# Running the first model's batches while the second model's weights are prepared

## Chip, cores and metric

One core of a Trainium2 chip runs one program on five engines: TensorE (PE), VectorE (DVE), ScalarE (ACT), GpSimd (POOL) and SyncE (SP), which only issues DMAs. Each engine works off its own instructions in their written order and waits on semaphores. The metric is the device time of one execution in microseconds (us).

## What is computed

Sixteen batches `x[b]` of 256 tokens by 256 features pass through two transformer blocks with conditioning, one after the other. Cut to what matters:

```python
# model 1, float32: cond = [t, c] @ Wc + bc -> a1, g1, be1, a2, g2, be2
h = layernorm(x) * (1 + g1) + be1
x = x + a1 * (softmax(h @ Wq @ (h @ Wk).T / 16) @ (h @ Wv))
h = layernorm(x) * (1 + g2) + be2
x = x + a2 * gelu(gelu(h @ W1 + b1) @ W2 + b2)          # W1: 256 x 1024, W2: 1024 x 256
# model 2: every linear has ternary weights and 8-bit activations
scale = 1 / max(mean(abs(w)), 1e-5); wq = clip(round(w * scale), -1, 1) / scale
# conditioning, once for all batches: six layers in a row on 16 rows
h = L(wa0, silu(c)); h = L(wa2, silu(gate) * y of L(wa1, h)); h = rmsnorm(L(wa3, h) + ba3)
s_msa, sc_msa, g_msa, s_mlp, sc_mlp, g_mlp = split(L(wa4, h) + ba4)   # wa4: 1536 x 1536
mx = layernorm(x) * (1 + sc_msa) + s_msa
i, f, g = L(wi, mx), sigmoid(L(wf, mx)), L(wg, mx)
o = scan over tokens of (f, silu(i) * (1 - f));  x = x + g_msa * L(wo, rmsnorm(o) * silu(g))
m = layernorm(x) * (1 + sc_mlp) + s_mlp;         x = x + g_mlp * L(wm2, silu(gate) * value of L(wm1, m))
```

Model 1 needs nothing of model 2's weights. Model 2 needs all six rows of its conditioning, and these need the mean of all of `wa4` before the first of its weights can be rounded.

## The kernel before

**Preparation.** It runs once, before the batches, and is written out by hand on each engine. SP loads the weights into `arena1` in groups (`load_group`, L321): `wa0` and `wa1`, then `Wc`, then `wa2` and `wa3`, then the block's own weights; after these, in place of them, the 12 chunks of `wa4` (128 x 1536 each, `wa4_chunk`, L294). For each weight there are three steps: a sum of absolute values (`absum_of`, ACT L561 or DVE L1117), summed over partitions by a matmul with ones (L1512) into `wmean` and `winv`; a multiplication by `winv` and addition of 12582912 that rounds (`w_round`, ACT L566 or POOL L414); and two operations of DVE that subtract this and clip (`ternary`, L1138 and L1140). The six conditioning layers (`LAYERS`) run between these steps, DVE doing their quantising (L1231 to L1248) and outputs, and the last one, `wa4`, takes its 12 chunks as they become ternary (L1573). Model 1's attention for batch 0 alone (`EARLY`) is woven into this by hand. At the end rows for all batches go to DRAM (`rows1_d`) and are read back per batch (`load_rows1`, `load_rows2`).

**Batches.** `run_pipeline` walks one list, `SCHEDULE`, of about 120 parts, each with a lag: in step k, part (name, lag) does batch k - lag. Model 1's parts have lags 0 to 3 (it ends with `x3`, DVE L945), model 2's first half lags 4 and 5 (`mx_a`, DVE L840, to `x4`), its second half lags 5 and 6 (to `x5`, POOL L518, and `store`). Steps 0 to 7 and the last six are written out; steps 8 to 15 are a loop on each engine with two steps per turn. `x3` has two buffers (`x3_sum` waits for `x4_ready` of two batches back, L944), so model 1 can't be more than two batches ahead of `x4`.

TensorE work per batch of model 1, all float32: 8 matmuls each for q (L1339), k (L1339), v, scores and attention output (L1346), 32 up (L1392), 32 down (L1401), each on 256 columns, and 16 transposes (L1326). Model 2's matmuls are bf16 (L1346, L1474), its transposes float16 and float32.

Of the kernel before, what the change touches and what calls it, by code (L numbers as in the profile page):

```python
# [5 lines left out]
SCHEDULE = [  # L6
    ("mx_a", 4), ("so_rstd", 5), ("sq_so", 5), ("q_mm", 2), ("vv", 5), ("k_mm", 2), ("u0", 6), ("silu0", 6),
    ("qT", 2), ("sq_o", 5), ("ln3_rstd", 4), ("z_o", 5), ("silu1", 6), ("gates1", 6), ("kT", 2), ("mx_b", 4),
    ("o_rstd", 5), ("z_i", 4), ("am_o", 5), ("u1", 6), ("xn2T", 3), ("quant_o", 5), ("val1", 6), ("a_rstd", 4),
    ("h2T", 3), ("gates2", 6), ("u2", 6), ("z_f", 4), ("am_i", 4), ("int_o", 5), ("u3", 6), ("am_f", 4), ("am_g", 4),  # L10
# [4 lines left out]
    ("v_mm", 2), ("load_x", 0), ("v", 2), ("u_rstd", 6), ("qT_f", 4), ("z_m", 5), ("down0", 3), ("qT_g", 4),  # L15
    ("g1", 3), ("int_f", 4), ("m_rstd", 5), ("round_i", 4), ("probT_mm", 2), ("my_b", 5), ("am_u", 6),
# [3 lines left out]
    ("quant_m", 5), ("sq_m", 5), ("ln2_rstd", 2), ("int_u0", 6), ("forget", 4), ("int_u3", 6), ("av_mm", 2),  # L20
# [4 lines left out]

EARLY = ("load_x", "load_rows0", "ln1_moments", "ln1_rstd", "ln1_norm", "xb", "xn1T", "hT", "q_mm", "qT", "k_mm", "kT",
         "v_mm", "v", "s_mm", "score_max", "exp", "probT_mm", "probT", "av_mm", "row_sums", "x2")


class Batch:


    def __init__(self, i, parity):
        self.i, self.p = i, parity

    def back(self, k):
        return Batch(self.i - k, (self.p + k) % 2)


def column(b):
    return slice(b.i, b.i + 1) if isinstance(b.i, int) else bass.ds(b.i, 1)


def wait(eng, sem, b, k=1, n=1, unit=1):

    value = b.i * (n * unit) + k * unit
    if isinstance(value, int) and value <= 0:
        return  # L50
    eng.wait_ge(sem, value)


def wait_dma(eng, sems, b):

    value = (b.i - b.p) * 8 + 16
    if isinstance(value, int) and value <= 0:
        return
    eng.wait_ge(sems[b.p], value)


def run_pipeline(eng, parts, schedule, nb):


    most = max(lag for _, lag in schedule)

    def step(k, parity):
        for name, lag in schedule:
            if isinstance(k, int) and (not 0 <= k - lag < nb or k == lag and name in EARLY):
                continue  # L70
            if name in parts:
                parts[name](Batch(k - lag, (parity + lag) % 2))

    first = most + 2
    first += (nb - first) % 2
    for k in range(first):
        step(k, k % 2)
    with eng.Fori(first, nb - 1, 2) as i:
        for w in range(2):
            step(i + w, (first + w) % 2)  # L80
    for k in range(nb, nb + most):
        step(k, k % 2)


def build_program(nc, t):
# [4 lines left out]
    P = 128  # L90
# [13 lines left out]
    with ctx:  # L104
# [29 lines left out]
        nrow = {n: sb("row_" + n, [P, D]) for n in ("ni", "nf", "ng", "ngn", "no", "nm1")}  # L134
        nrow["nm2"] = sb("row_nm2", [P, H])
# [18 lines left out]
        arena0 = sb("arena0", [P, 14752])  # L154
        arena1 = sb("arena1", [P, 18432])
# [15 lines left out]
        LOW, HIGH = 9 * T * D, 9 * T * D + 8608  # L171
        xin, rows0 = [take2(0, T, D)], [take2(0, 2, D)]
        xb, xn1, hT, qT, kT, v, prob = (take2(0, T, D) for _ in range(7))
        assert used[0] == LOW
        rows0.append(take2(0, 2, D))
        xn2, h2T = take2(0, T, D), take2(0, T, D)
        g = take2(0, HC, S)
# [110 lines left out]
        def tern_of(j):  # L288
            n = WNAMES[j]
            if n in AW:  # L290
                return AW[n]
# [1351 lines left out]
```

## Time and profile before

| | us |
|---|---|
| Time, median of 3 executions (lowest, highest) | 789.7 (788.61, 791.23) |
| The profiled execution's own time | 789.95 |
| Its span, first to last instruction | 788.1 |
| PE, DVE, ACT, POOL busy | 628.5, 620.6, 568.3, 458.3 |
| Share of PE, DVE, ACT, POOL | 80%, 79%, 72%, 58% |

The profile is of one execution. Busy time is the time in which at least one instruction of an engine was running; matmuls are pipelined, so that the ends of two neighbours overlap. PEclk is the share of its full clock that TensorE was granted: 1.0 is 2.4 GHz, 0.5 is 1.2 GHz.

### The profile page before, as it was taken

The page shows a single profiled execution, that of the slowest core. Times are in us where ns is not written, and L with a number is a line of the kernel's source. Part 1 is how long each engine was busy: PE and PEld are TensorE (multiplying, and loading weights), DVE is VectorE, ACT ScalarE, POOL GpSimd, SP SyncE. Part 2 cuts the span into 40 slices and gives each one's busy share as a digit, 9 for nine tenths or more (in the row PEclk, how much of TensorE's full clock was granted, in tenths as well). Part 3 has the DMA queues.
Part 4 walks back from the last instruction along what each step waited for, and adds up shares of the span by engine and source line. Part 5 has one row for each costly group of instructions (what it writes and reads, how often), then busy time and mean ns, then how long its engine had stood idle before and what let it go on. Part 6 is the DMA issues. An engine that isn't in the chain of part 4 may idle for free.

```text
span 788.1 us, 13091 instructions
## 1 busy us (share of the span) xinstructions
PE 628.5 (80%) x3560; PEld 487.7 (62%) x3588; DVE 620.6 (79%) x1432; ACT 568.3 (72%) x1206; POOL 458.3 (58%) x647
## 2 busy tenths in 40 slices
PE   0631336899899999999999999999999998874552
PEld 0110212678777878888787878788888877642321
DVE  3779888223768999999899989998899889888653
ACT  1234670447689999898989999998989888774431
POOL 2203360213647686867767686867678586856623
PEclk9955579799999999999999999999999999985866
DMA  8495800111010101202021011112021010110100
GB/s 312 150 408 204 297 0 25 30 38 47 1 68 35 46 37 48 68 15 68 13 67 47 33 47 47 37 43 66 14 67 34 22 40 22 49 34 1 34 14 14
DMA packets 17821, 51.96 MB, mean 66 GB/s; under 512 B 2880, under 2 KB 3712, under 8 KB 16880
## 3 DMA queue, kind: packets, MB, share of 16 engines
q1 hardware_dynamic: 17488, 50.92, 18.7%
q10 hardware_dynamic: 288, 0.52, 0.2%
q8 instruction: 19, 0.31, 0.2%
q14 instruction: 26, 0.21, 0.1%
HBM read 47.10 MB, written 4.33 MB: 65 GB/s over the span
## 4 chain that ended last, share of the span: by engine, by line
PE 58%; DVE 20%; issue 9%; POOL 5%; ACT 5%; DMA 2%; SPq 1%; DVEq 0%; POOLq 0%; ACTq 0%
PE bank L1346 15%; PE bank L1401 14%; PE bank L1339 7%; PE bank L1474 6%; PE bank L1326 5%; PE bank L1392 5%; DVE qa_dx L872 4%; PE bank L1318 2%; PE bank L1524 2%; PE bank L1489 2%; DVE arena L1138 2%; DVE qa_am L860 2%; DMA arena<-wo_dram 1%; POOL arena L512 1%; DVE arena L1009 1%
## 5 line engine op out<-in xcount | busy, mean ns | idle before, releaser
L1392 PE MATMUL bank<-arena,w 128*128 128x256 f32 x512 | 117.8, 379 | 0.0
L1401 PE MATMUL bank<-arena,w 128*128 128x256 f32 x512 | 116.7, 381 | 1.0 <-ACT arena L633 1.0
L1392 PEld LDWEIGHTS bank<-arena,w 128*128 128x128 f32 x512 | 96.1, 190 | 15.0
L1401 PEld LDWEIGHTS bank<-arena,w 128*128 128x128 f32 x512 | 94.9, 190 | 13.0 <-ACT arena L633 1.2
L1326 PE MATMUL bank<-ident,arena 128*128 128x128 f32 x448 | 66.9, 283 | 21.8 <-ACT arena L685 16.1
L1474 PE MATMUL bank<-tern_wm,qTm 128*128 128x512 bf16 x228 | 71.5, 403 | 15.1 <-ACT arena L707 6.2
L512 POOL TENSOR_TENSOR arena<-arena,row_nm 128x1024 f32<-128x1024 f32 x32 | 75.4, 2357 | 6.6 <-ACT junk_u L715 6.6
L1326 PEld LDWEIGHTS bank<-ident,arena 128*128 128x128 f32 x448 | 53.1, 145 | 35.1 <-issue 20.1
L694 ACT ACTIVATE arena<-arena,round_col,qa_qs 128x256 f32<-128x256 f32 x96 | 50.5, 592 | 22.4 <-DVE qa_qs L881 22.4
L1346 PE MATMUL bank<-arena 128*128 128x256 f32 x256 | 61.5, 383 | 3.1 <-DVE arena L899 3.1
L827 DVE BATCH_NORM_STATS2 ln_st<-arena 128x6 f32<-128x256 f32 x128 | 48.0, 417 | 18.1 <-POOL arena L502 11.7
L633 ACT ACTIVATE arena<-bank,b 128x256 f32<-128x256 f32 x128 | 51.4, 465 | 8.5 <-PE bank L1392 8.3
L1346 PEld LDWEIGHTS bank<-arena 128*128 128x128 f32 x256 | 47.1, 190 | 11.0 <-issue 2.9
L1040 DVE SCALAR_TENSOR_TENSOR arena<-bank,qm_dq,arena 128x512 f32<-128x512 f32 x64 | 47.8, 747 | 5.1 <-PE bank L1474 2.9
L707 ACT ACTIVATE arena<-bank,qm_dq 128x512 f32<-128x512 f32 x64 | 44.0, 687 | 10.1 <-PE bank L1474 9.6
L445 POOL TENSOR_TENSOR ln_ve<-ln_mv,eps_ln 128x2 f32<-128x2 f32 x32 | 7.1, 222 | 75.7 <-DVE ln_mv L832 75.7
L685 ACT ACTIVATE arena<-arena,ln_shift,ln_rstd 128x256 f32<-128x256 f32 x64 | 34.8, 591 | 15.6 <-POOL ln_shift L450 15.2
L1474 PEld LDWEIGHTS bank<-tern_wm,qTm 128*128 128x128 bf16 x256 | 21.7, 99 | 39.3 <-issue 26.8
L840 DVE SCALAR_TENSOR_TENSOR arena<-arena,ln_mv 128x256 f32<-128x256 f32 x64 | 41.4, 687 | 5.2 <-DVE ln_mv L832 1.9
L1318 PE MATMUL bank<-identh,arena 128*128 128x128 f16 x320 | 32.0, 224 | 14.8 <-DVE arena L1009 7.6
L488 POOL TENSOR_TENSOR arena<-arena,row_ngn 128x512 f32<-128x512 f32 x16 | 23.2, 1448 | 35.3 <-ACT arena L670 35.3
L518 POOL TENSOR_TENSOR arena<-arena 128x512 f32<-128x512 f32 x16 | 20.3, 1268 | 39.5 <-DVE arena L1009 39.5
(212 smaller groups left out, 1729.2 us busy)
## 6 DMA issues: line engine op xcount, KB each, us to landing
arena<-rows_d SPq DMA_DIRECT2D x32, 384.0 KB, 3.8
arena<-wa_dram SPq DMA_DIRECT2D x12, 768.0 KB, 10.0
arena<-x_dram SPq DMA_DIRECT2D x16, 256.0 KB, 2.6
arena<-rows_d SPq DMA_DIRECT2D x16, 256.0 KB, 3.4
out_dram<-arena SPq DMA_DIRECT2D x16, 256.0 KB, 2.0
arena<-Wc_dram SPq DMA_DIRECT2D x1, 3072.0 KB, 14.5
arena<-wm_dram SPq DMA_DIRECT2D x1, 2048.0 KB, 7.6
w<-W_dram SPq DMA_DIRECT2D x2, 1024.0 KB, 9.1
```

Source lines behind the costliest of these rows:

```text
L512: gp.tensor_tensor(u[:, k, :], u[:, k, :], nrow["nm2"][:, :], ALU.mult).then_inc(s["u2_ready"], 1)
L633: last = sc.activation(g[:, 2 * q + m, :], bank[3 - q % 2][:, m * S:(m + 1) * S], ACT.Gelu, bias=b1[:, 2 * q + m:2 * q + m + 1])
L694: last = sc.activation(z3[j][:, h, :], z3[j][:, h, :], ACT.Identity, bias=round_col[:, 0:1], scale=QN["a"]["qs"][:, j, h:h + 1])
L827: last = ve.bn_stats(st[:, j, :], src[:, j, :])
L1040: ve.scalar_tensor_tensor(out=u[:, k // 2, (k % 2) * 512:(k % 2 + 1) * 512], in0=bank[6][:, :], scalar=QN["m"]["dq"][:, 0, k // 2:k // 2 + ...
L1318: last = te.transpose(bank[bk_][:, :].bitcast(f16)[:, o:o + P], zh[:, b_, a * P:(a + 1) * P, 0], identh[:, :])
L1326: last = te.transpose(out[:, a * 256 + b_ * P:a * 256 + (b_ + 1) * P], src[:, b_, a * P:(a + 1) * P], ident_[:, :])
L1339: last = te.matmul(bank[bk_][:, m * S:(m + 1) * S], w[:, k, m * P:(m + 1) * P], x[:, k, :], start=k == 0, stop=k == C - 1)
L1346: last = te.matmul(bank[bk_][:, j * D:(j + 1) * D], xT[:, k, j * P:(j + 1) * P], w[:, k, :], start=k == 0, stop=k == K - 1)
L1392: last = te.matmul(bank[3 - q % 2][:, m * S:(m + 1) * S], w1[:, k, (2 * q + m) * P:(2 * q + m + 1) * P], h2T[:, k, :], start=k == 0, stop= ...
L1401: last = te.matmul(bank[3][:, c * S:(c + 1) * S], w2[:, k, c * P:(c + 1) * P], g[:, k, :], start=k == 0, stop=k == HC - 1)
L1474: last = te.matmul(bank[bk_][:, :], qTm[:, k, q // 2 * P:(q // 2 + 1) * P], tern["wm1"][:, k, col:col + 512], start=k == 0, stop=k == C - 1)
```

## The change

The list of steps with lags, the loop, `EARLY` and the hand-written preparation on each engine are gone. In their place stands `ORDER`, one written order of 2367 entries `name:batch`, in which every engine finds its parts of the preparation and of all 16 batches; nothing is a loop any more. In it batches 0 to 4 of model 1 stand among the preparation's parts.

```diff
-SCHEDULE = [
-    ("mx_a", 4), ("so_rstd", 5), ("sq_so", 5), ("q_mm", 2), ("vv", 5), ("k_mm", 2), ("u0", 6), ("silu0", 6),
...
+ORDER = """
+load_cond0 load_x:0 load_cond1 load_qkv load_g0 ada_c ada0_sq ada0_z vec2 ada0_r cond_mm0 vec3 ln1_moments:0 ada0_q
+ln1_rstd:0 ln1_norm:0 cond_f0 xn1T:0 hT:0 k_mm:0 cond_mm1 kT:0 rows0_turned cond_f1 q_mm:0 rows0_copy abs_wa0 abs_wa1
+store_rows0 qT:0 s_mm:0 load_rows0:0 load_x:1 load_rows0:1 load_mlp load_g1 v_mm:0 score_max:0 exp:0 sum0 xb:0 v:0 mean0
...
+s_mm:3 ada5_q v_mm:3 abs_a10 score_max:3 ada5_T gate2:1 exp:3 v:3 back:1 ada5_qT load_rows0:5 ln1_moments:4 abs_a11
+probT_mm:3 row_sums:3 ln1_rstd:4 x3:1 xn2T:2 probT:3 sum4 ln1_norm:4 av_mm:3 mean4 negated_gn h2T:2 ln1_moments:5 round_b0
...
+round_b11 tern_b9 back:2 qT:4 tern_b10 ada5_b9 s_mm:4 tern_b11 ada5_b10 score_max:4 ada5_b11 x3:2 v_mm:4 exp:4 ada5_y xn2T:3
+h2T:3 v:4 up0:3 store_rows1 row_sums:4 load_rows0:6 up1:3 g0:3 load_rows1:0 load_rows2:0 load_rows1:1 load_rows2:1
+probT_mm:4 g1:3 up2:3 probT:4 mx_a:0 up3:3 g2:3 mx_b:0 ln3_moments:1 sq_a:0 z_i:0 av_mm:4 g3:3 a_rstd:0 am_i:0 down0:3 x2:4
...
+yo:13 val0:12 x3:15 x5:11 load_rows2:13 gates0:12 gate_o:13 silu0:12 store:11 ln3_moments:15 qT_i:14 x4:13 load_rows1:15
...
+RING = 8
...
-    with eng.Fori(first, nb - 1, 2) as i:
-        for w in range(2):
-            step(i + w, (first + w) % 2)
...
+    for entry in order.split():
+        name, _, i = entry.partition(":")
+        if name in parts:
+            parts[name](Batch(int(i or 0)))
```

`x3` becomes a ring of 8 buffers. For the room, the seven row vectors share one tensor, the scratch tensors lie in `arena1`, and the DMA scratch is cut.

```diff
+        x3 = [take2(0, T, D) for _ in range(RING)]
...
-                wait(dve, s["x4_ready"], b.back(2))
-                ve.tensor_tensor(x3[b.p], halves(2), x2[b.p], ALU.add).then_inc(s["x3_ready"], 1)
+                wait(dve, s["x4_ready"], b.back(RING))
+                ve.tensor_tensor(x3[b.i % RING], halves(2), x2[b.p], ALU.add).then_inc(s["x3_ready"], 1)
...
-    nc = bacc.Bacc("TRN2", target_bir_lowering=False, num_devices=1)
+    nc = bacc.Bacc("TRN2", target_bir_lowering=False, num_devices=1, dynamic_dma_scratch_size=1024)
```

The weights still go through the same three passes. What changes is who makes them and from where. `wa4` has only seven slots: its 12 chunks pass through them once for their sums; the last seven stay, and the first five are loaded a second time. Rounding of `wa0` to `wa3`, `wm1` and all 12 chunks of `wa4` is ACT's; POOL rounds `wi`, `wf`, `wg`, `wo` and `wm2`, in pieces of 512 columns. DVE sums `wa1`, `wm1` and one chunk, ACT all others. `Wc` is multiplied with its own columns as the stationary operand, in two halves, so that its result comes out by features and needs no transposes.

```diff
+        SLOTS, WOVEN = 7, 5
+        KEPT = list(range(KC4 - SLOTS, KC4))
+        AGAIN = list(range(KC4 - SLOTS))
+        SECOND = KEPT + AGAIN
...
+        BY_DVE = ["wa1", "wm1", "a6"]
+        BY_ACT = ["wa0", "wa2", "wa3", "wi", "wf", "wg", "wo", "wm2"] + [f"a{i}" for i in range(KC4) if f"a{i}" not in BY_DVE]
...
+        ROUND_POOL = ["wi", "wf", "wg", "wo", "wm2"]
+        ROUND_ACT = ["wa0", "wa1", "wa2", "wa3", "wm1"] + [f"b{n}" for n in range(KC4)]
...
+            def rounded(n):
+                def part(_):
+                    place, j = rounding_place(pool, n)
+                    for o in range(0, place.shape[-1], 512):
+                        last = gp.tensor_scalar(place[:, o:o + 512], place[:, o:o + 512], winv[:, j:j + 1], MAGIC, ALU.mult, ALU.add)
+                    last.then_inc(s["wmagic_pool"], 1)
+                return part
...
+            def cond_mm(h):
+
+                def part(_):
+                    pe.wait_ge(s["feat_loaded"], 96)
+                    pe.wait_ge(s["qkv_loaded" if h else "cond_loaded"], 64 if h else 16)
+                    for m in range(3 * C * h, 3 * C * (h + 1)):
+                        for k in range(4):
+                            last = te.matmul(bank[5 - h][:, m * NB:(m + 1) * NB], wc[:, k, m * P:(m + 1) * P], tcT[:, k * NB:(k + 1) * NB],
+                                             start=k == 0, stop=k == 3)
+                    last.then_inc(s["cond_mm"], 1)
+                return part
```

## Rows read from the trace of the kernel before

**Rows 1.** Page, parts 1 and 2: engines' busy time, and 40 slices of the span
```profile
span 788.1 us, 13091 instructions
...
PE 628.5 (80%) x3560; PEld 487.7 (62%) x3588; DVE 620.6 (79%) x1432; ACT 568.3 (72%) x1206; POOL 458.3 (58%) x647
...
PE   0631336899899999999999999999999998874552
...
PEclk9955579799999999999999999999999999985866
```
**Rows 2.** Windows: stretch, its length, busy time and count per engine, clock, DMA
```profile
core 0: us, PE busy (x) PEld busy (x) DVE busy (x) ACT busy (x) POOL busy (x), PEclk, DMA share, GB/s
0.00:134.00 134.00, 51.33 (x180) 21.72 (x180) 99.64 (x160) 50.91 (x71) 39.55 (x44) 0.75 0.53 201
...
344.00:631.00 287.00, 280.29 (x1711) 232.57 (x1726) 260.29 (x636) 262.63 (x577) 209.40 (x300) 1.00 0.13 42
701.00:788.00 87.00, 39.41 (x200) 20.78 (x202) 54.08 (x114) 33.46 (x76) 45.86 (x55) 0.69 0.07 22
40.00:90.00 50.00, 11.37 (x50) 5.06 (x50) 41.93 (x84) 20.06 (x30) 12.63 (x12) 0.52 0.83 315
140.00:160.00 20.00, 18.27 (x72) 15.09 (x71) 3.94 (x19) 10.56 (x20) 4.73 (x13) 0.81 0.06 15
```
**Rows 3.** Single lines, x3's sum and x5's: duration min/median/max, first and last start
```profile
L945 DVE TENSOR_TENSOR arena<-bank,arena x16: 668/685/692, 172.6 to 700.8; 128x512 f32<-128x512 f32 x16
...
L518 POOL TENSOR_TENSOR arena<-arena x16: 1262/1268/1274, 273.1 to 784.3; 128x512 f32<-128x512 f32 x16
```
**Rows 4.** Groups by line and form, TensorE, 344 to 631 us
```profile
line engine op names shapes xcount | busy us, mean ns | idle before us <-releasers
...
L1392 PE MATMUL bank<-arena,w 128*128 128x256 f32 x256 | 59.2, 379 | 0.0
...
L1474 PE MATMUL bank<-tern_wm,qTm 128*128 128x512 bf16 x112 | 33.0, 379 | 0.8
...
L1326 PE MATMUL bank<-ident,arena 128*128 128x128 f32 x223 | 31.2, 274 | 0.0
...
L1339 PE MATMUL bank<-arena,wk 128*128 128x256 f32 x64 | 15.1, 379 | 0.0
```
**Rows 5.** Groups by line and form, ScalarE, whole span
```profile
L633 ACT ACTIVATE arena<-bank,b 128x256 f32<-128x256 f32 x128 | 51.4, 465 | 8.5 <-PE bank L1392 8.3
...
L616 ACT ACT_TABLE_LOAD x16 | 20.5, 1283 | 0.3
...
L561 ACT ACTIVATE arena<-arena 128x1536 bf16<-128x1536 f32 x8 | 11.9, 1482 | 4.4 <-DVE qa_am L1232 4.2
...
L566 ACT ACTIVATE arena<-arena,magic_col,winv 128x1536 f32<-128x1536 f32 x6 | 9.6, 1658 | 1.1 <-DVE winv L1130 1.1
...
L616 ACT ACTIVATION_READ_ACCUMULATOR arena<-bank,nbias 128x1 f32 x32 | 6.3, 196 | 0.0
```
**Rows 6.** Groups by line and form, VectorE, whole span
```profile
L827 DVE BATCH_NORM_STATS2 ln_st<-arena 128x6 f32<-128x256 f32 x128 | 48.0, 417 | 18.1 <-POOL arena L502 11.7 <-ACT arena L685 2.8 <-DMA arena<-x_dram 2.5
...
L1138 DVE TENSOR_SCALAR arena<-arena 128x1536 bf16<-128x1536 f32 x12 | 12.7, 1058 | 0.0
...
L1140 DVE TENSOR_SCALAR arena<-arena 128x1536 bf16<-128x1536 bf16 x12 | 10.3, 860 | 0.4
...
L918 DVE RECIPROCAL rinv<-rsum 128x2 f32<-128x2 f32 x16 | 2.5, 154 | 3.7 <-ACT arena L616 3.7
```
**Rows 7.** Timeline, 105 to 117 us: start, duration, instruction, idle time before it
```profile
103.61 12.00 POOL L414 TENSOR_SCALAR arena<-arena,winv 128x1536 f32<-128x1536 f32 x6 [9.62 <-DVE winv L1130]
...
107.52 1.78 DVE L1140 TENSOR_SCALAR arena<-arena 128x1536 bf16<-128x1536 bf16 x1
...
116.91 0.56 DVE L1140 TENSOR_SCALAR arena<-arena 128x1536 bf16<-128x1536 bf16 x1
```
**Rows 8.** Timeline, 0 to 17 us: DVE's first sum over a weight
```profile
11.96 3.89 DVE L1117 TENSOR_REDUCE absum<-arena 128x1 f32<-128x3584 f32 x1 [11.96 <-DMA arena<-wa_dram]
```

More of the change, by code:

```diff
@@ L62, in run_pipeline @@
[L62 to L77, printed above, removed]
-    with eng.Fori(first, nb - 1, 2) as i:
-        for w in range(2):
-            step(i + w, (first + w) % 2)
-    for k in range(nb, nb + most):
-        step(k, k % 2)
+    if value > 0:
+        eng.wait_ge(sems[b.p], value)
@@ L308, in walk @@
         def walk(eng, parts):
-            run_pipeline(eng, parts, SCHEDULE, NB)
+            run_pipeline(eng, parts, ORDER)
         @block.sync
@@ L551, in _ @@
+            for n in range(len(LAYERS)):
+                parts[f"ada{n}_r"] = ada_rstd(n)
+            for n in ROUND_POOL:
+                parts[f"round_{n}"] = rounded(n)
+            walk(pool, parts)
         @block.scalar
@@ L593, in part, with silu_hidden, evac_h @@
+            def silu_hidden(_):
+                act.wait_ge(s["ada_mm"], 2)
+                for k in range(2):
+                    last = sc.activation(hz[:, k * 448:(k + 1) * 448], bank[6 + k][0:NB, 0:448], ACT.Silu,
+                                         scale=QN["a"]["dq"][0:NB, 0, 0:1])
+                last.then_inc(s["ada_gate"], 1)
+            def evac_h(bk_, scale, shift, modulated, out, mm, ready, *free):
                 def part(b):
+                    if b.i == 0:
+                        act.wait_ge(s["cond_steps"], modulated)
+                        act.wait_ge(s["feat_loaded"], 96)
@@ L800, in _ @@
[L800 to L809 removed]
+            for n in range(len(LAYERS)):
+                parts[f"ada{n}_sq"] = square(n)
+            parts["ada_c"], parts["ada1_gate"] = silu_c, silu_hidden
@@ L811, in _ @@
+            for n in range(2, len(VEC)):
+                parts[f"vec{n}"] = load_vec(n)
+            for n in BY_ACT:
+                parts[f"abs_{n}"] = absum_of(n)
+            for n in ROUND_ACT:
+                parts[f"round_{n}"] = rounded(n)
+            load_vec(0)(None)
+            load_vec(1)(None)
+            act.dma_start(rows1_out[:, :], t["na4"].partition_broadcast(NB)).then_inc(s["na4_loaded"], 16)
+            act.wait_ge(s["consts_built"], 7)
             walk(act, parts)
@@ new lines, in with_bias, with ada3_out @@
+            def with_bias(out, w):
+                for k in range(3):
+                    last = ve.scalar_tensor_tensor(out=out[:, k * 512:(k + 1) * 512], in0=bank[COND_BANKS[k]][0:NB, :],
+                                                   scalar=q["dq"], in1=w[:, k * 512:(k + 1) * 512],
+                                                   op0=ALU.mult, op1=ALU.add)
+                return last
+            def ada3_out(_):
+                dve.wait_ge(s["ada_mm"], 4)
+                with_bias(hid, vec_of(5)).then_inc(s["ada_x"], 1)
+                dve.wait_ge(s["ada_x"], 5)
+                ve.tensor_copy(q["am"], q["dq"]).then_inc(s["vec_used"], 1)
@@ L1305, in _ @@
+            for n in (0, 1, 2, 3, 5):
+                parts[f"ada{n}_z"], parts[f"ada{n}_q"], parts[f"ada{n}_qT"] = ada_weighted(n), ada_quant(n), ada_evac(n)
+            for k in range(len(GROUPS) + 1):
+                parts[f"mean{k}"] = means(k)
+            for n in BY_DVE:
+                parts[f"abs_{n}"] = absum_of(n)
+            for n in TERNARY_ORDER + [f"b{k}" for k in range(KC4)]:
+                parts[f"tern_{n}"] = ternary(n)
             walk(dve, parts)
@@ new lines, in ada_turned, with part @@
+            def ada_turned(n):
+                def part(_):
+                    pe.wait_ge(s["ada_q"], min(n, 4) + 1)
+                    if n in (0, 5):
+                        pe.wait_ge(s["wmean_steps"], 4 if n else 1)
+                    for k in range(LAYERS[n][1] // P):
+                        last = te.transpose(bank[5][:, :].bitcast(bf16)[:, k * NB:(k + 1) * NB], qb[:, k * P:(k + 1) * P],
+                                            identb[0:NB, 0:NB])
+                    last.then_inc(s["ada_qT_mm"], 1)
+                return part
@@ new lines, in _ @@
+            parts |= {"cond_mm0": cond_mm(0), "cond_mm1": cond_mm(1), "rows0_turned": rows0_turned}
+            for k in range(len(GROUPS) + 1):
+                parts[f"sum{k}"] = sum_over_partitions(k)
+            for n in (0, 1, 2, 3, 5):
+                parts[f"ada{n}_T"] = ada_turned(n)
+            for n in range(4):
+                parts[f"ada{n}_mm"] = ada_mm(n)
+            for n in range(KC4):
+                parts[f"ada5_b{n}"] = ada5_mm(n)
+            pe.wait_ge(s["consts_built"], 6)
```

1047 lines of the change are left out of this document (555 added, 492 removed), and 11 rows, old and new, of the table SCHEDULE.

## The prediction, made before the changed kernel ran

> **What bounds the kernel now.** I read the page first. PE and DVE are busy for four fifths of the span and no engine for all of it; the 40 slices show where the rest is [rows 1]. PE is nearly idle in the first seven slices, full from about the ninth to the 35th, and half idle in the last five. So there are three stages, and the windows give each its numbers [rows 2]. Preparation, 0 to 134 us: DVE is busy for 99.6 us, PE for 51.3, at a mean granted clock of 0.75, and most of what PE does there is small work at half clock. Batches: over 344 to 631 us, which is eight of them, PE is busy for 280.3 of 287 us (98%), ACT for 262.6 and DVE for 260.3. This stage is PE's, at 35.9 us per batch, the others close behind. From x3 of the first to x3 of the last batch 528.2 us pass, 35.2 per batch [rows 3]. Tail: after x3 of the last batch at 700.8 us [rows 3] only model 2 is left, and the 87 us to the end hold 54.1 us of DVE and 39.4 of PE at a clock of 0.69 [rows 2].
>
> In steady state nothing can be gained without less PE work. What can be gained is PE's idle time in the preparation. Model 1 needs none of the weights that are prepared there, and it is the part that is heavy on PE.
>
> **What a batch costs each engine.** Model 1 has six groups of float32 matmuls in the steady window (L1392 the first, L1339 on wk the last), together 194.3 us, and four of the seven transposes of L1326, 17.8 of 31.2 us: 212.1 us, 26.5 per batch [rows 4]. All 15 groups add up to 318.2 us where PE was busy for 280.3, because the ends of bursts overlap the next one; shrunk alike, model 1 has 23.4. Its bursts are the longest and overlap least, so I take 24.6, and 35.0 - 24.6 = 10.4 for model 2. DVE: eleven groups of model 1 (half of L827 the first, L918 the last) sum to 109 us, 6.8 per batch [rows 6]; DVE has 32.5 in all, so model 2 has 25.7. ACT: eight groups (L633 the first, L616's read of the accumulator the last) sum to 176 us, 11.0 per batch [rows 5]; five table loads of 1.283 us make 6.4, and of 32.8 in all 15.4 are left for model 2's activations.
>
> **Leg 1, from the start to the first mx_a.** I counted what each engine finds in `ORDER` ahead of `mx_a:0`. Of model 1 it is 3.9 batches by PE's work, 4.3 by ACT's, 4.6 by DVE's.
> ACT: 11 sums over chunks of wa4 at 1.48 + 0.19 us are 18 us, the eight other sums, scaled by their columns, 11; 12 roundings of chunks at 1.66 are 20, the five others 13 [rows 5]; squares and gates of the conditioning 8, so 70. With 4.3 x 11.0 = 47 of model 1 and 11 table loads (14) it is 131 us. Before, ACT had 50.9 in its preparation [rows 2].
> DVE: 99.6, less 5 of batch 0's attention, less 8 for the sums that go to ACT, less 6 of waiting beside POOL (below), is 80; with 4.6 x 6.8 = 31 it is 111 us.
> PE: 51.3 x 0.75 - 9 of batch 0's attention is 30 at full clock [rows 2]; Wc's product gets shorter, so 25, and 3.9 x 24.6 = 96 makes 121 us.
> So the longest sum is ACT's. Before the first mean ACT has only 8 us of it. In the kernel before the first sum over a weight starts at 11.96 us with wa0 and wa1 landed [rows 8]; now Wc (3 MB) and q, k, v's weights are ahead of them, and I put the first mean at 25 us. Then 123 us of ACT remain. Without any idle time leg 1 would end at 148. But PE has to do its 121 us in the same time, and its clock won't be full: 0.81 where it is 91% busy from a cold start, 0.52 where it is 23% busy [rows 2]. At 0.85 they are 142 us, from about 12 us on, so no earlier than 154; and the six conditioning layers form a chain through all engines whose steps now queue behind instructions of model 1. I take 165, with 148 and 180 as the ends. That is later than the 134 of before, by 31 us: the price of the change.
>
> The second load of five chunks of wa4 is 3.8 MB. I cost it at nothing: it runs behind the seven kept chunks, whose roundings, clips and matmuls are its cover; DMA is 0.83 busy only in 40 to 90 us [rows 2]. Without that cover it would be about 12 us at that window's 315 GB/s. SP works in order too, and `load_x` of batches 4 and 5 stand among loads of chunks that wait for a slot; they are a batch ahead of their use, which covers a few us.
>
> POOL's roundings: while POOL rounded wa4, DVE's second clip took 1.78 us, and 0.56 when POOL had ended [rows 7]. Three such clips and the first subtraction make 5 to 6 us, and the group means above the undisturbed ones (1058 and 860 ns) show the same [rows 6]. These go, as ACT now rounds wa4. The Trainium skill ("SBUF — State Buffer", section "SBUF: two separate sides") says that GpSimd and VectorE lock a shared pair of ports for a whole instruction. By it POOL's short pieces of 512 columns cut the longest block to a third or less. The trace agrees with the lock for these clips.
>
> **Leg 2, to x3 of the last batch.** By the same count this stretch holds 12.0 batches of model 1 and 12.8 of model 2 on PE: 295 + 133 = 428 us. DVE: 11.4 x 6.8 + 13.4 x 25.7 = 422. ACT: 11.7 x 11.0 + 13.4 x 15.4 = 335, and 67 table loads of 1.283, 86, make 421. (In all the order needs 79 loads by my reading, against 76: 4 us more.) So the three are within 2%, where before PE led by 7%. With others that close PE was still 98% busy; here a stretch in which ACT or DVE is ahead costs PE time that isn't there again. I take 95% of PE: 428 / 0.95 = 451 us. The ends are 98%, 437, and 90%, 476. The loop that goes was worth little: PE idled 6.7 us in all of 287 us that it nearly covers [rows 2]. The Trainium skill ("Runtime: NRT & Kernel Launch", section "Instruction fetch mechanics") says that a taken branch can stall the fetch and straight code is fetched ahead; by it up to those 6.7 us could come back, 2% of leg 2, inside my ends.
>
> The wait that the ring takes away (x3 for x4 of two batches back) isn't long in the trace; the ring's use is that model 1 may lead by four batches at the first mx_a. What is late next is model 2: from leg 1's end its 16 batches need 411 us of DVE alone.
>
> **Leg 3, the tail.** At x3 of the last batch the new order still owes all of batch 15, most of 14, batch 13 from its first residual on, and the MLP half of 12: 2.65 batches of DVE, 68 us, against 54.1 in the tail before [rows 2]. That tail idled DVE for 33 us, since the last batches are chains; one more batch beside them fills part. 68 + 27 = 95 us. Ends: 87, as now, and 104.
>
> **The sum.** 165 + 451 + 95 = 711 us of span. The profiled execution took 789.95 at a span of 788.1, so 1.9 us lie around it, and it stands 0.25 us above the median of 789.7. So 713 us.
>
> **Rivals.**
> A. The packing succeeds: ACT has no idle time in leg 1, PE 98% in leg 2, a tail as now. 148 + 437 + 87 + 2 = 674. For it: such a steady state exists in the trace. Against it: no stretch of the preparation has any engine that full.
> B. Three full engines hold each other up: whoever is late in one written order makes the other two late. Leg 2 at 88%, 486 us, leg 1 at 178: 178 + 486 + 95 + 2 = 761. For it: the sums lie within 2%, and some stretches hold up to 43 us of ACT for one batch. Against it: 95% and more was reached with 91% on two others.
> C. Slower than before: PE stays at its lower level in leg 1. In 40 to 90 us the clock is 0.52 [rows 2], and if model 1's bursts come with as many pauses between waits for ACT and DVE, 121 us of PE become 242, leg 1 ends near 254, and the sum is 802. It decides from a leg 1 of 242 us on, a mean clock of 0.53. Against it: PE has work for over 80% of the leg, and at 91% busy the clock was 0.81.
> D. The change doesn't do what it says: batches 1 to 4 of model 1 sit in the order, but don't run in PE's idle time, since each stands behind a part of the preparation that waits. Leg 1 would then take the old 134 plus most of 96 us of PE, 215, and the sum would be 763. The in-order queues speak for it; that the parts alternate closely speaks against.
>
> **Chances.** Forecast (685 to 750) 0.72, A below 685 0.08, B and D above 750 but faster 0.15, C 0.04, about no change 0.01. A measurement of this kernel can tell 0.3% from no change. Faster 0.95, same 0.01, slower 0.04. The range for 8 in 10 is 685 to 750.
>
> **What would show it.** First start of L840's counterpart (mx_a) at 150 to 180 us, x3 of batch 2 before it; PE's slices 3 to 9 at 7 or more; PEclk there above 0.8; x3 of the last batch at 600 to 640; DVE and ACT both above 90% between. DVE's clips at 0.95 and 0.56 us throughout. Wrong would be: mx_a after 200 us with PE's slices low (D), or low clock (C), PE below 90% in the middle with no engine above 95% (B). If the last x3 to the end takes over 105 us, the tail was read wrongly.

## The result: slower, and the profile after

The changed kernel takes 812.9 us (median; 812.4 to 817.1), the kernel before 790.0 in the same session; the ratio is 1.030, with an interval of 1.026 to 1.034. The forecast was 713 us, faster by 10%, with 0.04 for slower. The page of the changed kernel, parts 1 and 2, answers to [rows 1]:

```profile
span 811.4 us, 12653 instructions
...
PE 653.5 (81%) x3626; PEld 505.4 (62%) x3650; DVE 619.6 (76%) x1424; ACT 587.9 (72%) x1219; POOL 442.1 (54%) x646
...
PE   4969798998989897989889885799799986845442
...
PEclk9989899999999999999999998999989999958765
```

PE's idle front has gone, as intended: its slices read 4 9 6 9 7 9 8 where they read 0 6 3 1 3 3 6 [rows 1]. But the block of nines behind them has gone too. Below are the three legs of the forecast as windows (columns as in [rows 2]), and then the lines that bound them: x3's sum, x5's sum, the line whose first instruction is `mx_a:0`, and the reciprocal of a weight's mean ("the first mean" and so on below):

```profile
0.00:181.00 181.00, 147.89 (x669) 116.59 (x670) 107.24 (x252) 121.76 (x188) 39.25 (x89) 0.95 0.53 192
181.00:700.00 519.00, 454.00 (x2670) 359.81 (x2689) 437.62 (x1024) 423.32 (x932) 344.04 (x488) 0.98 0.11 36
700.00:811.00 111.00, 51.59 (x290) 29.02 (x292) 74.74 (x150) 42.85 (x99) 58.76 (x69) 0.72 0.08 27
```
```profile
L1110 DVE TENSOR_TENSOR arena<-bank,arena x16: 660/680/692, 89.8 to 700.1; 128x512 f32<-128x512 f32 x16
...
L733 POOL TENSOR_TENSOR arena<-arena x16: 1262/1270/1654, 272.3 to 807.6; 128x512 f32<-128x512 f32 x16
...
L1005 DVE SCALAR_TENSOR_TENSOR arena<-arena,ln_mv x64: 452/478/2583, 180.8 to 766.6; 128x256 f32<-128x256 f32 x64
...
L1297 DVE RECIPROCAL winv<-wmean x5: 164/166/179, 47.9 to 139.1; 128x2 f32<-128x2 f32 x3, 128x4 f32<-128x4 f32 x1, 128x1 f32<-128x1 f32 x1
```

Leg 1 took 181 us (forecast 165), leg 2 519 (451), leg 3 111 (95): 100 us in all. Most of it is in leg 2, where PE was busy for 87% of the time. The last x3 stands where it stood before, at 700 us [rows 3]: 3.9 batches of lead at the first mx_a were worth nothing at the last x3.

A second way of cutting the span is of more use below, because model 2 ends it: the first mx_a, from there to the first x5, and from the first x5 to the last. Before, that is 174.5 + 98.6 + 511.2 us; after, 180.8 + 91.5 + 535.3. So model 2, whose first step began 6 us later than before, needed 35.7 us per batch, where it had needed 34.1.

### The profile page after: what moved, and what is told of

Same layout as the page of the kernel before. It is cut to its first block and busy times, and to the rows that moved or that the text cites. A ratio compares the mean times of both kernels' runs of the same rounds, so it can differ in the third digit from the quotient of the medians.

```text
span 811.4 us, 12653 instructions
## 1 busy us (share of the span) xinstructions
PE 653.5 (81%) x3626; PEld 505.4 (62%) x3650; DVE 619.6 (76%) x1424; ACT 587.9 (72%) x1219; POOL 442.1 (54%) x646
## 5 line engine op out<-in xcount | busy, mean ns | idle before, releaser
L1546 PEld LDWEIGHTS bank<-arena,w 128*128 128x128 f32 x512 | 95.4, 190 | 17.8 <-ACT arena L845 5.0
L1465 PE MATMUL bank<-ident,arena 128*128 128x128 f32 x448 | 70.8, 285 | 33.0 <-DVE arena L1154 13.9
L727 POOL TENSOR_TENSOR arena<-arena,rows 128x1024 f32<-128x1024 f32 x32 | 77.2, 2412 | 34.0 <-ACT arena L927 33.8
L1621 PE MATMUL bank<-tern_wm,arena 128*128 128x512 bf16 x232 | 67.9, 384 | 25.8 <-ACT arena L919 10.9
L694 POOL TENSOR_TENSOR arena<-arena,rows 128x512 f32<-128x512 f32 x48 | 61.6, 1298 | 22.6 <-DVE arena L1015 22.6
L1485 PE MATMUL bank<-arena 128*128 128x256 f32 x256 | 65.2, 400 | 8.4 <-ACT arena L819 4.4
L1636 PE MATMUL bank<-identh,arena 128*128 128x128 f16 x256 | 24.1, 243 | 43.0 <-DVE arena L1053 32.8
L862 ACT ACTIVATE arena<-arena 128x256 bf16<-128x256 f32 x96 | 39.2, 418 | 21.2 <-DVE arena L1015 14.6
L1005 DVE SCALAR_TENSOR_TENSOR arena<-arena,ln_mv 128x256 f32<-128x256 f32 x64 | 47.6, 790 | 7.0 <-DMA arena<-rows_d 6.4
L1621 PEld LDWEIGHTS bank<-tern_wm,arena 128*128 128x128 bf16 x256 | 21.3, 97 | 49.4 <-issue 37.1
L1636 PEld LDWEIGHTS bank<-identh,arena 128*128 128x128 f16 x256 | 18.7, 108 | 49.8 <-DVE arena L1053 35.7
```

Of the source, the lines that this page charges most:

```text
L694: gp.tensor_tensor(z3[j], mx, over_tokens(nrow[("ni", "nf", "ng")[j]]), ALU.mult).then_inc(s["z3_ready"], 1)
L727: gp.tensor_tensor(u[:, k, :], u[:, k, :], nrow["nm2"], ALU.mult).then_inc(s["u2_ready"], 1)
L1005: last = ve.scalar_tensor_tensor(out=out[:, j, :], in0=src[:, j, :], scalar=mv[:, j, 0:1], in1=rows[:, 1, :], op0=ALU.subtract, op1=ALU.mult)
L1465: last = te.transpose(out[:, a * 256 + b_ * P:a * 256 + (b_ + 1) * P], src[:, b_, a * P:(a + 1) * P], ident_[:, :])
L1485: last = te.matmul(bank[bk_][:, j * D:(j + 1) * D], xT[:, k, j * P:(j + 1) * P], w[:, k, :], start=k == 0, stop=k == K - 1)
L1546: last = te.matmul(bank[3][:, c * S:(c + 1) * S], w2[:, k, c * P:(c + 1) * P], g[:, k, :], start=k == 0, stop=k == HC - 1)
```

## Experiments

**Is it the written order?** The first run keeps the changed kernel up to `mx_a:0` and lets the old step follow, with model 2 two steps later than there.

```diff
-ORDER: everything behind mx_a:0, 2001 entries by hand
+def regular(order, lead, first):            # lead 2, first 4
+    for k in range(first, 16 + 6 + lead):
+        for name, lag in SCHEDULE:          # of the kernel before
+            i = k - lag - (0 if name in MODEL1 else lead)
+            ...                             # f"{name}:{i}", if not there yet
```

> The changed kernel, with its written order kept up to the first mx_a; from there on the steps of the old list follow in their old sequence, with model 2's parts two steps later than there (so model 1 keeps its lead of two batches more, to its end). Parts, buffers, ring and preparation are the same. Theory O (the sequence of the parts in the written order costs the time, by making engines wait for each other): the middle leg, first mx_a to last x3, falls from 519 us to 12 steps of 33 to 36 us, about 425, PE is 96% busy or more in it, the tail is the old 87 us plus two batches of model 2 alone at 28 us, so about 181 + 425 + 143 + 2 = 751 us, below the kernel before. Theory R (three engines that are nearly equally full hold each other up whatever the sequence): PE stays at 82 to 88% in the middle, the time at 790 us or above.

Measured: 788.9 us (785.8 to 792.0), ratio to the kernel before 0.999 (0.997 to 1.001). Its windows, with leg 2 and 3 by its own x3:

```profile
181.00:634.00 453.00, 427.84 (x2590) 351.96 (x2589) 385.46 (x942) 393.17 (x866) 310.90 (x445) 0.98 0.12 38
634.00:787.00 153.00, 75.87 (x394) 40.78 (x394) 107.81 (x232) 67.39 (x160) 90.98 (x113) 0.65 0.08 26
...
262.00:370.00 108.00, 105.97 (x655) 88.09 (x654) 98.37 (x244) 99.56 (x219) 79.85 (x115) 1.00 0.13 45
```

In three steps of the middle PE is busy for 106 of 108 us; over 252 to 378 us the changed kernel had it busy for 112.63 of 126 us at a clock of 0.99. So 24 of the 100 us are the order behind `mx_a:0`. But neither theory had the total. Leg 2 is now 453 us, near the forecast of 451, only because less of model 2 lies in it (385.5 us of VectorE, where 422 were counted and the changed kernel had 437.6); what it leaves stands in the tail, forecast at 95 us and now 153. Five batches of model 2 are unfinished at the last x3. The first three x5 behind it follow at 32 to 33 us each, the last two, with ever less beside them, at 28 and 23.

One part of what the order costs can be read. Behind the first mx_a both kernels run the same 1173 instructions on VectorE, but these keep it busy for 512.5 us in the hand-written order and for 493.2 in the regular one. A line of model 1 shows how (median 348 and 346 ns, but up to 1356 in the first and 354 in the second), and the timeline of the changed kernel has a case:

```profile
L1104 DVE TENSOR_SCALAR arena<-arena,cond x32: 329/348/1356, 88.5 to 698.3; 128x256 f32<-128x256 f32 x32
```
```profile
L1008 DVE TENSOR_SCALAR arena<-arena,cond x32: 320/346/354, 88.6 to 631.5; 128x256 f32<-128x256 f32 x32
```
```profile
309.60 1.61 DVE L1104 TENSOR_SCALAR arena<-arena,cond 128x256 f32<-128x256 f32 x2
309.76 1.30 POOL L733 TENSOR_TENSOR arena<-arena 128x512 f32<-128x512 f32 x1 [2.76 <-DVE arena L1174]
...
311.27 0.66 PE L1465 MATMUL bank<-ident,arena 128*128 128x128 f32 x4 [0.98 <-DVE arena L1104]
```

The pair of VectorE's instructions, 0.61 us elsewhere, ends 0.15 us after POOL's sum does, and PE waits for it. The regular order has such places too (one line of small VectorE instructions takes 1766 ns on average in it and 539 in the hand-written one), but fewer in all. How much of the 24 us this is wasn't tried.

**Is it the loop, or ScalarE as a third full engine?** Three runs: the kernel before with its `Fori` written out (`for k in range(nb + most): step(k, k % 2)`), and both kernels with Gelu, Silu and Exp replaced by Tanh, so that hardly a table is loaded.

> The kernel before with its loop of four turns written out, nothing else changed. Theory L (straight code is fetched worse than a loop whose code is there, and that is part of the changed kernel's loss): slower by 1% or more. Otherwise (the loop was worth nothing either way): within 0.3% of 790 us, at most 7 us faster if the turns had cost anything.

Measured: 787.6 us, ratio 0.998 (0.996 to 0.999).

> The changed kernel with every Gelu, Silu and Exp replaced by Tanh, so that other functions than the reference's are computed and ScalarE loads a table once or twice instead of 77 times: some 96 us less on ScalarE. Theory R (equally full engines): ScalarE was one of three, PE gets back to 90% or more in the middle leg, the time falls by 40 us or more. Theory O: the waits are for the sequence, and ScalarE's loads are one of many lengths in it: 10 to 30 us less.

Measured: 805.9 us, ratio 1.023 (1.019 to 1.027).

> The kernel before with every Gelu, Silu and Exp replaced by Tanh, so that other functions than the reference's are computed and nearly no table is loaded. Both theories: its middle is PE's at 98%, so nothing is gained there; the tail's chains lose a few loads, 3 to 10 us less in all. It is the measure for what the same edit does to the changed kernel.

Measured: 787.8 us, ratio 0.997 (0.995 to 0.998). Part 1 of the changed kernel's page without tables:

```profile
PE 653.5 (81%) x3650; PEld 504.6 (63%) x3650; DVE 618.6 (77%) x1424; ACT 490.6 (61%) x1143; POOL 441.6 (55%) x646
```

ScalarE has 97 us less to do than in the changed kernel (587.9), and the kernel is only 7 us faster. Rival B as I wrote it, three engines within 2% that hold each other up, would have given most of leg 2's loss back once one of them is at 61%; PE was busy for 458.6 of the 519 us from 181 to 700, 88% as before. Seven us are also less than the 10 to 30 that the other theory allowed. The kernel before gains 2 us. So it is not how full ScalarE is that holds the hand-written order up. With the regular step's 24 us, what is left is who waits for whom in it. Straight code alone is worth 2 us of 790, within the forecast's bound of 6.7.

**Is the lead worth its price?** Model 1's parts ahead of `mx_a:0` are thinned to what the old steps 0 to 3 have (batch 0 whole, batch 1 up to `ln2_norm`, batch 2 up to `hT`, not to v as the expectation says), and `regular` runs with lead 0.

```diff
-... xn2T:1 h2T:1 up0:1 ... x3:1 ... s_mm:2 ... x3:2 ... up3:3 ... probT:4 mx_a:0     # ahead of mx_a:0
+ORDER = regular(ORDER, 0, 4)                # those entries now come in their steps
```

> The changed kernel's preparation with only as much of model 1 in it as the kernel before has of it by the first quantization of model 2 (batch 0 whole, batch 1 to its attention's end, batch 2 to its v, batch 3's first moments), then the kernel before's order of a step for both models, with no lead of model 1. Theory: a lead of model 1 earns nothing at the end, and what it takes of ScalarE and VectorE (about 1.9 batches at some 16 us of ScalarE each, 30 us) lengthens the preparation. Then leg 1 falls from 181 to about 155, the rest takes 607 to 613 us as in the kernel before and in the regular order with a lead of two, and the whole takes about 768, faster than both kernels. Rival: the preparation is bound by its own chain of weights, behind a first mean at 48 us, and model 1 lies beside it for free: leg 1 stays at 175 to 180, the whole at 785 to 790.

Measured: 776.8 us (775.6 to 778.6), ratio 0.984 (0.982 to 0.986): faster than both kernels. Its x5 and mx_a lines, and the regular kernel's:

```profile
L630 POOL TENSOR_TENSOR arena<-arena x16: 1262/1272/1279, 264.2 to 773.0; 128x512 f32<-128x512 f32 x16
...
L902 DVE SCALAR_TENSOR_TENSOR arena<-arena,ln_mv x64: 471/482/1392, 164.4 to 737.0; 128x256 f32<-128x256 f32 x64
```
```profile
L637 POOL TENSOR_TENSOR arena<-arena x16: 1261/1268/1272, 278.5 to 784.0; 128x512 f32<-128x512 f32 x16
...
L909 DVE SCALAR_TENSOR_TENSOR arena<-arena,ln_mv x64: 471/482/1392, 181.5 to 746.5; 128x256 f32<-128x256 f32 x64
```

Cut at the first mx_a and the first x5 again, with the lead: 181.5 + 97.0 + 505.5 us. Without: 164.4 + 99.8 + 508.8. The lead makes the preparation 17.1 us longer and gives 6.1 back. (Two later runs with the same preparation as the regular kernel have their first mx_a at 178.8 and 184.7 us, so the 17 are good to some 3 us.) Leg 1 fell less than I expected (155), so something else holds it at 164; the next runs look for that.

**What holds leg 1?** First, the sums, mean and rounding of `wa0` and `wa1` ahead of the second half of Wc's product, in the changed kernel and in the one without lead.

```diff
-... k_mm:0 cond_mm1 kT:0 rows0_turned cond_f1 q_mm:0 rows0_copy abs_wa0 abs_wa1 ... sum0 ... mean0 ... round_wa0 ... round_wa1
+... k_mm:0 abs_wa0 abs_wa1 sum0 mean0 round_wa0 round_wa1 cond_mm1 kT:0 rows0_turned cond_f1 q_mm:0 rows0_copy ...
```

> The changed kernel with the sums, the mean and the rounding of its first two weights placed ahead of the second half of Wc's product, all else as it was. The first mean was due at 25 us by the prediction and came at 47.9; if leg 1 is long (181 us) because the preparation started late, the first mean comes near 30, leg 1 shrinks by about the same 18 us to 163, and the whole gives about 795. If leg 1 is held by the work of model 1's batches that stands among the weights (ScalarE is busy for 113.7 of the 133 us from 48 to 181), the first mean moves by 18 us and leg 1 by no more than about 5: about 808.

Measured: 810.4 us (808.1 to 814.8), ratio 1.027 (1.023 to 1.032). The first mean came at 28.4 us instead of 47.9, and mx_a at 180.0 instead of 180.8: the second theory, whether or not its reason holds.

> As the kernel with no lead of model 1, and the first two weights' sums, mean and rounding ahead of the second half of Wc's product. Theory (work bound in leg 1): without the extra batches the chain of weights becomes what is late, so that the earlier mean now counts: leg 1 about 145, the whole about 758. Rival: as without the move, within 4 us of it.

Measured: 777.6 us (772.8 to 778.0), ratio 0.984 (0.980 to 0.987). First mean at 28.6, mx_a at 164.6, where it was 164.4: the rival. Then, on top of this, the loads:

```diff
-load_g0 ada_c ... store_rows0 ... load_rows0:0 load_x:1 load_rows0:1 load_mlp load_g1
+load_g0 load_mlp load_x:1 ada_c ... load_g1 store_rows0 ... load_rows0:0 load_rows0:1
```

> The kernel with no lead of model 1 and the early first mean (777.6 us), with three loads moved up in SyncE's written order: W1 and W2, which wait for nothing, right behind the first two weights (the DMA engines stand still from 24 to 44 us), and the third and fourth weight ahead of the store of the first rows. Theory: leg 1 (165 us here) is held by the loads of wa2, wa3 and what follows, which are issued at 43.6 us because they wait for the end of Wc's product and stand behind the store; they then share the DMA engines with 2 MB of W1 and W2. Then the second mean comes at about 56 instead of 66, and leg 1 falls by 5 to 10 us, the whole to about 769. Rival: what follows the third mean (wa4's twelve pieces, each a transfer, a rounding and two passes of VectorE) holds leg 1: no change within 3 us.

Measured: 777.9 us (777.0 to 779.0), ratio 0.984 (0.981 to 0.988); mx_a at 164.4, the rival again.

> The changed kernel with the same moves (first mean early, W1, W2, wa2 and wa3 loaded earlier), its own written order in all else. If its leg 1 (181 us) is bound by the work of model 1's batches on ScalarE, nothing: 807 to 813. If the loads held it, leg 1 falls by 5 to 10 us: about 802.

Measured: 815.5 us (808.9 to 817.7), ratio 1.033 (1.030 to 1.037), mx_a at 179.3. Nothing either. The timeline of ScalarE in the kernel without lead and with earlier loads says why the second mean stayed at 65 us; SyncE had issued wa2 and wa3 at 35.3:

```profile
57.04 1.02 ACT L707 ACTIVATE arena<-bank,mod_shift,mod_scale 128x256 f32<-128x256 f32 x2 [3.76 <-PE bank L1362]
57.95 1.69 ACT L654 ACTIVATE arena<-arena 128x1792 bf16<-128x1792 f32 x1
...
61.71 2.75 ACT L654 ACTIVATE arena<-arena 128x3072 bf16<-128x3072 f32 x1
```

L654 is the sum of `wa2`; it follows at once on L707, `hT` of batch 1, which had waited 3.76 us for PE. So the sum stood behind model 1 in ScalarE's order. Does that cost anything at the end? Two runs on top of that kernel move parts of model 1 out of the way: all of them from the first mean on behind the second, or those of batches 1 to 3 behind the fourth.

```diff
-mean0 ... [batch 0's attention, batch 1's first parts among them] ... abs_wa2 ... abs_wa3 ... sum1 mean1
+mean0 ... abs_wa2 ada1_qT abs_wa3 sum1 mean1 kT:0 q_mm:0 qT:0 s_mm:0 v_mm:0 ...
```

> As the kernel with no lead of model 1 and the earlier loads (777.9 us, leg 1 of 164, second mean at 65 us), with the preparation up to its second mean placed ahead of batch 0's attention in the one written order. In that kernel wa2 has landed long before 58 us, but its sum starts on ScalarE at 57.95 us, right behind batch 1's scaling (hT), which waits 3.8 us for TensorE. Theory: the written order, not work or loads, holds the preparation behind batches 0 and 1. Then the second mean comes at about 50 and leg 1 ends 8 to 12 us earlier, the whole at about 768. Rival: batch 0's own chain is as long as what stands before it, and comes out later by what the preparation gains: leg 1 within 3 us of 164, the whole 775 to 780.

Measured: 782.8 us (779.8 to 787.5), ratio 0.992 (0.990 to 0.995). The second mean moved from 65 to 50 us, the third from 104 to 108, and mx_a from 164.4 to 168.1.

> The same, but batch 0's parts stay where they are among the preparation, and all parts of batches 1 to 3 that stood before the fourth mean (105 us) come behind it. Theory: the fourth mean moves ahead by what batches 1 to 3 held it up, 10 to 15 us, and the batches' parts still fit beside wa4's chunks, so that leg 1 gets 5 to 10 us shorter: 768 to 773. Rival: the parts pile up behind the mean and lengthen the rest of leg 1 by as much: 777 or more.

Measured: 798.6 us (796.2 to 799.5), ratio 1.012 (1.009 to 1.015). The fourth mean moved from 105 to 100 us, the fifth from 134 to 153, mx_a to 183.5. The theory fell both times, and the loss is larger than either rival had it (780 us at most; the second only set a lower end): a mean that comes earlier is paid back behind it. Work taken out does help, as the next run shows, the kernel without lead with half of Wc's terms left out.

```diff
-                        for k in range(4):      # cond_mm
+                        for k in range(2):
```

> The kernel with no lead of model 1 (776.8 us), with half of Wc's product left out (two of the four terms of each sum, 96 of 192 matmuls of 16 columns, about 10.3 us of TensorE). Theory: the product of 192 narrow matmuls, 20.7 us in which TensorE mostly loads weights, holds up the loads that take Wc's place, so that leg 1 gets about 8 to 10 us shorter: about 768. Rival: its time is covered by what leg 1 waits for later, and nothing changes (774 to 779).

(The counts in that expectation are off: the product has 48 matmuls in the code and 96 records in the trace, and half of each was left out. A float32 matmul leaves two records; the counts of model 1's matmuls given for the kernel before are records too, and the code has half as many, 4 for q and 16 for up.) Measured: 768.8 us (765.2 to 770.5), ratio 0.972 (0.968 to 0.976). The product in the kernel without lead, this run's, and its mean and mx_a lines:

```profile
L1573 PE MATMUL bank<-arena 128*128 128x16 f32 x96 | 20.6, 372 | 11.6 <-DMA arena<-Wc_dram 11.6
```
```profile
L1573 PE MATMUL bank<-arena 128*128 128x16 f32 x48 | 10.4, 371 | 11.3 <-DMA arena<-Wc_dram 11.3
```
```profile
L1194 DVE RECIPROCAL winv<-wmean x5: 164/166/178, 37.3 to 124.6; 128x2 f32<-128x2 f32 x3, 128x4 f32<-128x4 f32 x1, 128x1 f32<-128x1 f32 x1
...
L902 DVE SCALAR_TENSOR_TENSOR arena<-arena,ln_mv x64: 471/484/1396, 154.7 to 727.7; 128x256 f32<-128x256 f32 x64
```

10.2 us of PE less, and the rest of leg 1 comes 9.7 us earlier: first mean 47.0 to 37.3, last mean 134.4 to 124.6, mx_a 164.4 to 154.7. The median falls by 8.0 us, from 776.8 to 768.8. So the half that was left out lay on the path nearly whole.

**Why does model 2 alone take 33 us per batch?** In the regular kernel, the chain of waits over one of these steps (the longest pieces: start, length, what):

```profile
663.77 3.41 issue
667.22 1.26 POOL arena L637
...
671.43 1.88 PE bank L1525 x4
...
676.37 2.49 POOL arena L598 x2
678.86 2.30 POOL arena L631
...
682.32 1.27 POOL arena L621
683.58 2.31 POOL arena L631
...
688.42 1.26 POOL arena L626
...
690.97 4.96 issue
695.97 1.27 POOL arena L607
697.24 2.35 issue
699.62 1.27 POOL arena L637
```

L637 is x5; from one to the next are 32.4 us. POOL's instructions are 17.8 of them: the products with the rows ni, nf and ng of the norms (L598), with nm2 for u (L631), with nm1 for m (L626) and with ngn for the gate (L607), x4 (L621), and the small sums and roots between. PE, DVE and ScalarE together have 3.7, and 10.7 are time in which the profile shows no releaser. The two longest of these gaps stand ahead of L607 and x5; by POOL's waits over 640 to 740 us it sat idle ahead of L607 for ScalarE (15.0 us in three times) and ahead of x5 for DVE (8.9 in three). Its busy time is 66.6 of 100 us, DVE's 80.0. One run raises PE's clock, one takes work off POOL:

```diff
+            def warm(n, m):                    # 6 before qT_i and qT_u0, 2 before gates0, last five steps
+                ...
+                    for k in range(n):
+                        te.matmul(bank[0][:, 0:D], wq[:, 0, 0:P], wq[:, 1, :], start=True, stop=True)
```

> The regular order with a lead of two (788.9 us), whose last five batches of model 2 run alone at 33 us each with TensorE busy for 54% at a mean granted clock of 0.66 to 0.68. Here fp32 products of 128 x 256 into a free bank, read by nobody, stand in TensorE's gaps of those five steps: six before the first turn of z and of u, two before the gates; they cost about 0.43 us each at the full clock. If the half clock is what makes a batch of model 2 alone take 33 us, the granted clock after 634 us rises above 0.9, a step falls to about 28 us and the whole to about 766. If the chain through VectorE, ScalarE and GpSimd sets it (VectorE is busy for 80%), the clock rises and the steps stay at 32 to 34: 787 to 794.

```diff
-                    gp.tensor_tensor(u[:, k, :], u[:, k, :], nrow["nm2"], ALU.mult)
+                    w = H if b.i < 11 else P
+                    gp.tensor_tensor(u[:, k, 0:w], u[:, k, 0:w], nrow["nm2"][:, 0:w], ALU.mult)
```

> The regular order with a lead of two (788.9 us); in the last five batches GpSimd's product of u with nm2 (twice 2.31 us a batch) is done for 128 of the 1024 columns, about 0.35 us each, the rest left as it was, so that about 3.9 us of GpSimd's work is left out in a batch. The chain of waits from 664 us on lies on GpSimd's queue nearly without a break (13 products, roots and sums, two gaps of 5.0 and 2.4 us). If GpSimd's written order sets the period of model 2 alone, each of the last five steps falls from 33 to about 29 us and the whole to about 770. If TensorE's half clock or VectorE (80% busy) sets it, steps stay above 32: 784 to 789.

Measured: 781.6 us (780.7 to 786.8) and 778.7 (776.0 to 781.1), ratios 0.992 (0.990 to 0.995) and 0.985 (0.981 to 0.989). The window from 640 to 740 us in the regular kernel, with the fillers, and with less work for POOL:

```profile
640.00:740.00 100.00, 53.83 (x296) 30.37 (x296) 80.01 (x175) 52.55 (x130) 66.58 (x86) 0.66 0.08 28
```
```profile
640.00:740.00 100.00, 72.39 (x393) 47.64 (x390) 81.42 (x180) 51.44 (x125) 70.48 (x86) 0.83 0.09 28
```
```profile
640.00:740.00 100.00, 59.05 (x305) 32.44 (x308) 78.80 (x185) 56.15 (x137) 62.07 (x92) 0.68 0.10 32
```

From x5 of batch 10 to x5 of batch 15 pass 150 us in the regular kernel, 145 with the fillers at a clock of 0.83, and 138 without most of POOL's product. So this rise of the clock is worth 1 us a step; what the full clock would be worth isn't shown. POOL's work falls by 3.8 us a batch (ten pieces of 0.46 us in place of 2.36), and a step by 2.4 of the 4 that I expected. Both times lie between the two theories of the expectation. What the runs show is that neither the clock nor this product alone sets the period, and that no engine is full. That it is one chain through all engines in their written orders is the reading left, argued from the chain above. Whether another order of model 2 alone would get it nearer to DVE's 25.7 us wasn't tried.

## Why the prediction was wrong, point by point

**Model 2's period** is the term that decided, in "What is late next is model 2: from leg 1's end its 16 batches need 411 us of DVE alone". I priced a batch of model 2 at its busiest engine's work, 25.7 us. Alone it takes 32 to 33 (33.3, 28.2 and 21.8 us for the last three x5 before, which were there to be read), and beside model 1 35.8. From the first mx_a the span needs about 97 us to the first x5 and 15 steps. The regular kernel shows this with PE at 98% in its middle steps: it still takes 606 us behind its first mx_a, where 546 were forecast. So of the 100 us that the forecast missed, 60 stand behind the first mx_a whatever the order, nearly all of them 15 steps at 33.7 us (505.5 / 15) where the forecast left 30; 24 are the hand-written order and 16 leg 1. (That the regular kernel's leg 2 and PE's work in it, 453 and 427.8 us, meet the forecast's 451 and 428 is chance: it holds less of model 2.) A batch of lead turns one step of 35.8 us into one of 33, which is why two batches of lead bought 6.1 us. The forecast of 711 - 165 = 546 us behind the first mx_a leaves, with 97 us to the first x5, 30 us for each of 15 steps; no stretch of the trace before had shown that beyond the drain of the last two batches.

**Leg 2** at 95% of PE was 87%: 454.0 of 519 us. PE's work was 26 us more than the 428 counted, DVE's 437.6 for 422, ScalarE's 423.3 for 421. The step "I take 95% of PE: 428 / 0.95 = 451 us" took for the hand-written order a share that only the old step had shown; the old step in its place gives 24 us back. Rival B had the share (88%) and gave 761. Its cause, full engines, fell with the run without table loads. What it said beside this, that whoever is late in one written order makes the others late, is what the runs leave.

**Leg 1**: 181 us, one above the end of the range. Busy times were near: ScalarE 121.8 for 131, DVE 107.2 for 111, PE 147.9 for 142. PE's is luck: at the measured clock of 0.95 it is 140 us of work at full clock where 121 were counted, and the clock, put at 0.85, hid it. The first mean came at 47.9 instead of 25 us, which I would have blamed; two runs show that it cost nothing. What was wrong is "Wc's product gets shorter, so 25", for which no row of the kernel before spoke: 24 records of 12.5 us on PE before the batches became 96 records of 20.7, and batch 0 now waits for them. Half of them was worth 9.7 us of leg 1; that the whole is worth 20 is extrapolated. The lead's work was the other part, about 17 us. So the preparation was neither bound by ScalarE's sum nor free for model 1: it is a chain that grows by part of what is woven into it. I had also weighed 165 against 134, the end of the preparation before. The stretch that answers to leg 1 ended at 174.5 us there, so even the forecast gained only 9 us in it. What the chain consists of between the second and the fourth mean stays open; three moves of order didn't shorten it.

**Leg 3** held 74.7 us of DVE for the forecast's 68 and 36 idle for 27: 111 for 95, past the 105 I had named as the sign that the tail was misread.

**Right**: PE's front fills, its clock there is above 0.8; x3 of batch 2 (171 us) before the first mx_a; 77 table loads for 79; straight code worth almost nothing. DVE's clips of wa4 with POOL out of the way: 

```profile
L1322 DVE TENSOR_SCALAR arena<-arena 128x1536 bf16<-128x1536 f32 x12 | 12.1, 1006 | 5.3 <-ACT arena L764 5.2
L1324 DVE TENSOR_SCALAR arena<-arena 128x1536 bf16<-128x1536 bf16 x12 | 6.8, 564 | 0.4
```

The second pass is at 564 ns on average for 860 in [rows 6], which is the 0.56 of [rows 7], and the first at 1006 for 1058: 4.1 us of DVE for the 5 to 6 of the forecast. That the end of the span moved by it isn't shown. By the exclusive lock on a shared pair of ports that the Trainium skill ("SBUF — State Buffer", section "SBUF: two separate sides") describes, such a pass waits for a POOL instruction that holds the ports. The trace agrees: the twelve second passes take 0.56 to 0.58 us now that ScalarE rounds wa4, eleven of the first ones 0.94 to 0.96, and the one beside a product of POOL (142.13 to 143.40 us) 1.55. Of the stalls at taken branches that the Trainium skill ("Runtime: NRT & Kernel Launch", section "Instruction fetch mechanics") warns of, the run with the loop written out shows at most its 2.4 us of 790; no trace tells whether they were such stalls. Rival C wasn't near (clock 0.95). D has a part in it: model 1's batches did run early, and made the preparation later.

## What to carry to other kernels

Filling the idle time of the busiest engine is worth only what the second chain behind it can use: before moving work ahead of a stage, read that chain's own period from a stretch where it runs alone (here the last steps of the tail), and not from the sum of its busiest engine. Then weigh a lead by its two prices, what it adds to the stage that it is woven into (about 8.5 us per batch of lead here), and what one step shrinks by when the work is gone (35.8 to 33 us). Keep a regular order where it already holds the bound engine at 98%: a hand-written one lost 24 us here with the same parts.

## What the runs showed of the hardware

- This float32 product isn't cheaper with the wide matrix as the stationary operand, though it has few columns to move. Wc's product takes 20.7 us in 96 records with 16 columns, and took 12.5 us in 24 with Wc as the moving operand of 512 columns (L1524 before). Weight loads fill it as much as matmuls do, as the changed kernel's rows from 0 to 50 us show (PE, then PEld), and the window over its second half (clock 1.00):

```profile
L1676 PE MATMUL bank<-arena 128*128 128x16 f32 x96 | 20.7, 372 | 11.7 <-DMA arena<-Wc_dram 11.7
```
```profile
L1676 PEld LDWEIGHTS bank<-arena 128*128 128x128 f32 x96 | 20.8, 333 | 11.8 <-issue 11.6
```
```profile
27.00:38.00 11.00, 11.00 (x52) 10.81 (x51) 0.88 (x2) 0.00 (x0) 0.00 (x0) 1.00 0.01 1
```

  That is one load of 128 x 128 float32 in 0.212 us over this window (10.81 us for 51), and 0.217 over all 96. The Trainium skill ("TensorE: Matmul & The Clock Gate", section "LDWEIGHTS (loading the stationary operand)") gives the columns divided by 1.2, in ns, with no word of their type; for 128 columns that is an estimate of 107 ns. The measured time in this product is twice that, and it decides.
- Fillers in PE's gaps raised the granted clock of a half-idle stage from 0.66 to 0.83, for 5 us of 150: in this stage, where PE was busy for 54% of the time, that much of the clock was worth 1 us a step.
